# The rounds of attention written out in a new order: values' product first, q and k product in two pieces, high and low parts one round later, hT in three buffers

## The reference

```python
h = layernorm(x); h = h * (scale + 1) + shift          # scale, shift, gate from the condition
q, k, v = split_heads(h @ w_qkv)                       # 16 heads of 16
q = rope(layernorm(q, q_norm_w)); k = rope(layernorm(k, k_norm_w))
attn = softmax(q @ k.T / 4)                            # per batch and head, 256 x 256
x = x + (attn @ v) @ w_out * gate
```

## Time and profile before

| | before |
|---|---|
| median of 3 runs | 1654.78 us (1653.81 to 1656.48) |
| profiled execution | 1659.2 us, span 1657.6 us |
| TensorE busy, share of the span | 1313.8 us, 79% |
| VectorE busy | 855.8 us, 52% |
| ScalarE busy | 645.3 us, 39% |
| GpSimd busy | 324.6 us, 20% |
| mean granted clock of TensorE | 0.890 |

### The profile page before, as it was taken

The page is one execution under the profiler, slowest core; times in us unless marked ns, Lnnn a source line. Parts: engine busy times, 40 slices in busy tenths (PEclk is TensorE's granted clock), DMA queues, the critical chain, the costliest instruction groups (busy, mean ns, idle before and its releaser), DMA issues. The chain is left out here.

```text
span 1657.6 us, 37130 instructions
## 1 busy us (share of the span) xinstructions
PE 1313.8 (79%) x15240; PEld 1035.8 (62%) x15240; DVE 855.8 (52%) x1946; ACT 645.3 (39%) x1205; POOL 324.6 (20%) x311
## 2 busy tenths in 40 slices
PE   2378887887888755445149999999998999999997
PEld 2245655655656422112049999999998888888885
DVE  3656556556555245555565565655654334433432
ACT  1155565565554445544413233323322233223332
POOL 2252342442433134444300000000000000000000
PEclk8589898898897887777559999999999999999998
DMA  8112112112112300000047888888883000000000
GB/s 320 53 39 78 39 38 77 38 39 77 39 39 77 102 0 0 0 0 0 0 203 305 340 347 334 340 353 326 345 335 125 9 16 15 16 10 16 16 15 16
DMA packets 37880, 188.06 MB, mean 113 GB/s; under 512 B 3056, under 2 KB 13424, under 8 KB 29040
## 3 DMA queue, kind: packets, MB, share of 16 engines
q1 hardware_dynamic: 37744, 186.10, 29.4%
HBM read 160.66 MB, written 25.17 MB: 112 GB/s over the span
## 5 line engine op out<-in xcount | busy, mean ns | idle before, releaser
L1023 ACT ACTIVATE g<-ph,b 128x256 f32<-128x256 f32 x256 | 121.5, 475 | 276.5 <-PE ph L1186 276.4
L813 PE MATMUL pg<-XT,wfih_sb 128*128 x192 | 117.6, 777 | 102.8 <-DVE logs L898 101.0
L546 DVE TENSOR_REDUCE mx<-pR 128x4 f32<-128x1024 f32 x128 | 155.6, 1222 | 70.9 <-PE pR L673 69.6
L1376 DVE STREAM_TRANSPOSE preT<-pr 128x64 f32<-128x64 f32 x256 | 64.1, 250 | 223.8 <-PE pr L1274 223.8
L1200 PE MATMUL py<-ghi,w 128*128 128x256 f32 x512 | 147.5, 288 | 20.5 <-issue 16.2
L437 ACT ACTIVATE probs<-pR 128x1024 f32<-128x1024 f32 x128 | 131.7, 1030 | 77.0 <-PE pR L682 76.8
L1184 PE MATMUL ph<-xhi,w 128*128 128x256 f32 x512 | 146.5, 286 | 17.9 <-DMA w<-weight_halves 17.9
L1131 DVE CAST ghi<-g 128x256 fp32r<-128x256 f32 x256 | 74.8, 292 | 156.8 <-ACT g L1023 156.6
L813 PEld LDWEIGHTS pg<-XT,wfih_sb 128*128 128x128 f32 x192 | 47.4, 257 | 172.8 <-issue 172.8
L1350 ACT ACTIVATE hs<-preT 128x32 f32<-128x32 f32 x256 | 58.8, 230 | 228.6 <-DVE preT L1376 228.6
L1185 PE MATMUL ph<-xlo,w 128*128 128x256 f32 x512 | 146.0, 285 | 0.0
(11 more groups left out here) (189 smaller groups left out, 3006.5 us busy)
## 6 DMA issues: line engine op xcount, KB each, us to landing
w<-weight_halves SPq DMA_DIRECT2D x66, 2048.0 KB, 12.0
weight_halves<-wparts SPq DMA_DIRECT2D x40, 512.0 KB, 4.0
modw<-in_ew SPq DMA_DIRECT2D x32, 256.0 KB, 4.3
xn<-in_x_tok SPq DMA_DIRECT2D x4, 1024.0 KB, 12.0
XT<-in_x_dm SPq DMA_DIRECT2D x2, 2048.0 KB, 14.0
out_dm<-staged SPq DMA_DIRECT2D x16, 256.0 KB, 2.1
modw<-in_sw SPq DMA_DIRECT2D x8, 256.0 KB, 4.2
modw<-in_mod_w SPq DMA_DIRECT2D x1, 768.0 KB, 7.4
```

The source lines that it names most:

```text
L546: nc.vector.reduce_max(mx[:, :, 2 * j:2 * j + 2].rearrange("p t s -> p s t"), pR[k][:].rearrange("p s (t k) -> p s t k", t=TC), AX.X).then ...
L813: i = nc.tensor.matmul(pg[u][:, g], wfih[:, c, g * D + u * P:g * D + (u + 1) * P], XT[:, c, bass.ds(2 * p, 2)], start=(c == 0), stop=(c == ...
L1023: nc.scalar.activation(g[:, t % RING], ph[t % RING][:, 0:T], ACT.Gelu_apprx_tanh, bias=b1[:, n, f:f + 1]).then_inc(gelu_done, 1)
```

## The change

The list of fills gets a new order, all 20 rounds are written out for every engine, and each engine gets an order of its own in place of following the list:

```diff
-FILLS = [("scores_max", 0, 1), ("scores_max", 1, 1), ("scores", 0, 0), ("scores_max", 2, 1), ("scores", 1, 0),
-         ("norm_rows", 0, -1), ("scores_max", 3, 1), ("scores", 2, 0), ("out_rows", 0, -1), ("scores_max", 4, 1), ("scores", 3, 0),
-         ("project", 0, -1), ("scores_max", 5, 1), ("scores", 4, 0), ("scores_max", 6, 1), ("scores", 5, 0), ("qk_raw", 0, 3),
+FILLS = [("scores_max", 0, 1), ("scores_max", 1, 1), ("scores", 0, 0), ("norm_rows", 0, -1), ("scores_max", 2, 1), ("scores", 1, 0),
+         ("scores_max", 3, 1), ("scores", 2, 0), ("out_rows", 0, -1), ("scores_max", 4, 1), ("scores", 3, 0), ("qk_raw", 0, 3),
+         ("scores_max", 5, 1), ("scores", 4, 0), ("scores_max", 6, 1), ("scores", 5, 0), ("project", 0, -1),
          ("scores_max", 7, 1), ("scores", 6, 0), ("scores", 7, 0)] + [("qk_rows", i, 2) for i in range(4)]
-        hT = sb(st, "hT", [P, 2, DC, T])
+        hT = sb(st, "hT", [P, 3, DC, T])
```

TensorE (the waits inside are as before):

```diff
+                if has(r, 1):
+                    values_of(r + 1)
+                maxima(0)
+                maxima(1)
+                weights(0)
+                if has(r, -1):
+                    rows_of_o()
+                maxima(2)
+                weights(1)
+                if has(r, 3):
+                    rows_of_x(r + 3)
+                maxima(3)
+                weights(2)
+                if has(r, -1):
+                    out_rows()
+                maxima(4)
+                weights(3)
+                if has(r, 3):
+                    qk_raw(r, 0)
+                maxima(5)
+                if has(r, 3):
+                    qk_raw(r, 1)
+                weights(4)
+                maxima(6)
+                weights(5)
+                if has(r, -1):
+                    project()
+                maxima(7)
+                weights(6)
+                weights(7)
+                if has(r, 1):
+                    rows_of_max()
...
+                    rows_of_qk(r, 0)
+                    rows_of_qk(r, 1)
+                if has(r, 0):
+                    values(QUADS - 1)
+                if has(r, 2):
+                    rows_of_qk(r, 2)
+                    rows_of_qk(r, 3)
```

ScalarE (each line stands under its `has`):

```diff
+                    copy_v(r + 1, 1 - par)
+                    exponential(r, 0)
+                    high_parts(r)
+                    exponential(r, 1)
+                    modulate(r + 3)
+                    exponential(r, 2)
+                    save(r, 0)
+                    more_high_parts()
...
+                    nc.scalar.copy(oT[:].rearrange("p c t -> p (c t)"), pR[k][:, 0]).then_inc(free[k], 1)
...
+                    exponential(r, 3)
+                    save_raw(r)
+                    exponential(r, 4)
+                    save(r, 1)
+                    squares(r)
+                    exponential(r, 5)
+                    exponential(r, 6)
+                    save(r, 2)
+                    root(r + 3)
+                    exponential(r, 7)
+                    max_row(r)
+                    evacuate_qk(act, nc.scalar.copy, r, par, 1)
+                    evacuate_qk(act, nc.scalar.copy, r, par, 3)
...
                     save(r, QUADS - 1)
```

VectorE (the same; `scale_qk` now waits for `ya_ready` of the batch before in place of its `slots_pool`):

```diff
+                    normalise(r + 3)
+                    maxima(r, 0)
+                    maxima(r, 1)
+                    divide(r)
+                    for j in range(2, 7):
+                        maxima(r, j)
...
                     sums_of_squares(r + 3)
...
+                    add_projection(r)
+                    maxima(r, 7)
+                    negated_maxima(r)
+                    evacuate_qk(dve, nc.vector.tensor_copy, r, par, 0)
+                    scale_qk(r + 3)
+                    evacuate_qk(dve, nc.vector.tensor_copy, r, par, 2)
+                if r == -3:
                     for q in range(1, 4):
                         dve.wait_ge(x_in[q], 16)
                         token_norms(4 * q, 4 * q + 4)
```

GpSimd: the rotation of batch r+3 is at the end of round r, and the low parts of batch r+2 at its start:

```diff
                 if has(r, 2):
-                    rotate(r + 2)
+                    low_parts(r + 2)
                 for n in range(2 * (r + 3), 2 * (r + 4)):
                     split_piece(pool, n)
+                if has(r, 3):
+                    rotate(r + 3)
...
             def rotate(b):
...
                 pool.wait_ge(y_ready, b + 1)
-                if later(b):
+                if b > 0:
                     pool.wait_ge(slots_act, 3 * b)
+                    pool.wait_ge(slots_pool, b)
```

More of the change, by code:

```diff
@@ L243, in attention @@
         qk_groups = qkraw[:].rearrange("p t (g e) -> p (t g) e", e=HD)
[L244 to L258, removed]
+        ROUNDS = range(-3, B + 1)
         def has(r, ahead):
-            return not isinstance(r, int) or 0 <= r + ahead < B
+            return 0 <= r + ahead < B
         def await_full(eng, r, kind, j=0):
@@ L310, in _ @@
                 load_piece(sp, n)
-            rounds(None, one)
+            for r in ROUNDS:
+                one(r, r % 2)
             sp.wait_ge(max_moved, 32 * B)
@@ L350, in rotate, with low_parts @@
                 nc.gpsimd.tensor_tensor(yav, yav, yb[:].rearrange("p t q h j -> p (t q) h j"), ALU.add).then_inc(ya_ready, 1)
+                assert s.n == 3, s.n
+            def low_parts(b):
                 pool.wait_ge(hi_ready, b + 1)
[L353 to L357, removed]
+                nc.gpsimd.tensor_tensor(slots[:, :, 0, :, HD:2 * HD], ya[:, :, 0], slots32[:, :, 0, :, 0:HD], ALU.subtract).then_inc(half_low, 1)
+                nc.gpsimd.tensor_tensor(slots[:, :, 1, :, 2 * HD:3 * HD], ya[:, :, 1], slots32[:, :, 1, :, 0:HD], ALU.subtract)\
+                    .then_inc(slots_pool, 1)
+            for r in ROUNDS:
+                one(r, r % 2)
         @block.scalar
@@ L463, in one @@
+                if has(r, 0):
+                    exponential(r, 7)
+                if has(r, 1):
+                    max_row(r)
+                if has(r, 2):
+                    evacuate_qk(act, nc.scalar.copy, r, par, 1)
+                    evacuate_qk(act, nc.scalar.copy, r, par, 3)
                 if has(r, 0):
                     save(r, QUADS - 1)
-            rounds(act, one)
+            for r in ROUNDS:
+                one(r, r % 2)
         @block.vector
@@ new lines, in add_projection @@
+            def add_projection(r):
+                await_full(dve, r, "project")
+                dve.wait_ge(xT_in, 48)
+                k = bank_of("project")
+                for c in range(DC):
+                    xv = XT[:, c, r - 1]
+                    i = nc.vector.scalar_tensor_tensor(out=xv, in0=pR[k][:, 0, c * T:(c + 1) * T],
+                                                       scalar=modT[:, 2 * DC + c, r - 1:r], in1=xv, op0=ALU.mult, op1=ALU.add)
+                    i.then_inc(half_projected if c == 0 else free[k], 1)
@@ L599, in scale_qk @@
                 assert s.n == ROOT - 1, s.n
-                if later(b):
-                    dve.wait_ge(slots_pool, b)
+                if b > 0:
+                    dve.wait_ge(ya_ready, b)
                 nc.vector.tensor_tensor(y[:].rearrange("p t q h e -> p (t q h) e"), qk_groups,
                                         rs[:].unsqueeze(2).broadcast_to([P, TC * 2 * HEADS, HD]), ALU.mult).then_inc(y_ready, 1)
-            rounds(dve, one)
+            for r in ROUNDS:
+                one(r, r % 2)
         @block.tensor
@@ L633, in rows_of_x, with values_of @@
                 i.then_inc(x_rows, 1)
-            def values_of(b, par, last):
-                pe.wait_ge(hT_ready, b + 1 if last else b + 2)
-                if later(b):
+            def values_of(b):
+                pe.wait_ge(hT_ready, min(b + 2, B))
+                if b > 0:
                     pe.wait_ge(v_ready, b)
@@ L641, in values_of, with qk_raw @@
                     for c in range(DC):
-                        i = nc.tensor.matmul(pA[:, t * D:(t + 1) * D], hT[:, par, c, t * P:(t + 1) * P], wqkv[:, c, 2 * D:3 * D],
+                        i = nc.tensor.matmul(pA[:, t * D:(t + 1) * D], hT[:, b % 3, c, t * P:(t + 1) * P], wqkv[:, c, 2 * D:3 * D],
                                              start=(c == 0), stop=(c == DC - 1))
                 i.then_inc(v_done, 1)
-            def qk_raw(r, par):
-                bank, done = filling(r, "qk_raw")
-                pe.wait_ge(hT_ready, r + 4)
-                if not later(r + 3):
-                    pe.wait_ge(dve_ready, 2)
-                for t in range(TC):
-                    for c in range(DC):
-                        i = nc.tensor.matmul(bank[:, t], hT[:, par, c, t * P:(t + 1) * P], wqkv[:, c, 0:2 * D],
-                                             start=(c == 0), stop=(c == DC - 1))
-                i.then_inc(done, 1)
+            def qk_raw(r, t):
+                if t == 0:
+                    filling(r, "qk_raw")
+                    pe.wait_ge(hT_ready, r + 4)
+                    if r + 3 == 0:
+                        pe.wait_ge(dve_ready, 2)
+                k = bank_of("qk_raw")
+                for c in range(DC):
```

(42 more changed lines are left out.)

186 lines of the change are left out of this document (76 added, 110 removed).

## The result

The changed kernel takes 1636.0 us (median of 4, 1635.0 to 1637.7) against 1654.3: a ratio of 0.9888, 95% interval 0.9871 to 0.9905. It is faster, but by 18 us and not by the 66 forecast, and it lies outside the range. The profiled execution took 1636.7, its span is 1635.1 us, 22.5 less than before. The spans differ by more than the medians, because the profiled execution of the kernel before was 4.4 us above its median.

The account below looks back on a forecast made before the run. A round was taken as bound by the TensorE-VectorE handshake, not by an engine. Savings of 44.4 + 3.5 + 4.5 + 3 + 11 = 66.4 us gave 1588.4 us by the median; range 1573 to 1604, to 1626 with rival A.

Parts of the forecast that it names:

- normalising 0.64: VectorE at the head of a new round: normalising takes 0.64 us, read from the old trace.
- the layout of the new round: Times of one full round on all engines: 26.7 us with 2.8 of waiting, taken as 27.1 with small gaps.
- TensorE waits 0.55: Head of the new round: TensorE waits 0.55 us for reduction 0, ending at 3.55, before transposing oraw.
- rival C: Slower: rotation beside VectorE's normalising and reductions takes twice its 5.3 us, round 34.6, total 1690 us; chance 0.04.
- Full rounds: Rounds 1 to 12: each falls from 30.8 to 27.1 us, 44.4 us saved in all.
- rival A: The clock goes on falling once a round: rounds of 27.1 + 2.7, less 0.3 to 0.8, total 1624 us; chance 0.20.
- The ramp: Before round 0: token norms move behind scale_qk(0), so round 0 starts near 89.1 for 100.9; 11 us taken.
- They then run 33 to 51, beside GpSimd: In the ramp: the moved token norms, 18.1 us, run from 33 to 51 us while GpSimd splits and rotates.
- Round 0: First round of attention, without oraw transposes, output rows or projection: 27.5 to 23.7 us, 3.5 taken.
- Round 13: Round without qk product or rows of x: from 28.9 to between 23 and 25 us, 4.5 taken.
- At no cost: Moves of wx and wh loads, row of maxima and low parts cost nothing; nothing taken for leaving out the loops.
- Rivals B and C: B: only the ramp gains; rotation 2.5 us longer, high_parts late, round stays 30.8, total 1643 us; chance 0.06.

Follow-up runs that it names:

- e1: Changed kernel with VectorE normalising batch r+4 behind the negated maxima, not r+3 at the round's head: 1592.1 us, ratio 0.9605 to the kernel before.
- e5: As e1, with the token norms of batches 4 to 15 in one call instead of three: 1582.9 us, ratio 0.9565 to the kernel before.
- e9: Changed kernel with normalising as scalar_tensor_tensor instead of tensor_scalar at the same place: 1645.7 us, ratio 0.9939 to the kernel before.

## Why the prediction was wrong

**The step that failed** is the term "normalising 0.64" in the layout of the new round. By it VectorE was free at about 1.1, before the first maxima were ready, so that normalising lay under the values' product at no cost and "TensorE waits 0.55". Normalising takes 3.2 us there, because the same layout had put GpSimd's rotation at -0.7 to 4.6, over it, and TensorE waits 2.2. The duration was read from the earlier trace rows, where GpSimd stood still. A row gives a duration in its surroundings, and the surroundings were part of the edit.

The prediction came near it in rival C. It asked whether rotation would grow beside normalising, cited the Trainium skill ("GPSIMD Engine Reference", "1. Specifications") that GpSimd shares its SBUF interfaces with VectorE, noted that no row showed the two together, and then priced the wrong side. The runs show VectorE to wait and GpSimd to be delayed by 0.05. What this section of the Trainium skill names is VectorE instructions with two SBUF inputs or in a two-port mode. In these runs `tensor_tensor` and `scalar_tensor_tensor` with two SBUF inputs waited, which agrees; `tensor_scalar` with two scalar columns waited too, and no row tells whether it ran in a two-port mode. C's own sum is also off: 27.1 and 5.2 are 32.3 a round, not 34.6, unless the clock falls as well, which it doesn't say.

**Full rounds**: 44.4 forecast, 17.9 in the span. Of the 26.5 missing, by rounds without a fall of the clock, 12 x (28.2 - 26.9) = 15.6 are the wait itself, and 12 x (29.3 - 28.2) = 13.2 the clock, which falls in seven of twelve rounds behind the longer wait; 2.4 come back, as the layout was slower by 0.2 a round than e1 (26.4 in all). So rival A happened as a consequence and in part, not in its own right: at e1's waits the clock holds, with the same three banks in turn. That A's round (27.1 + 2.7, less 0.3 to 0.8) comes near the 29.3 measured is luck, as its sum leaves the long wait out. Without the contention the layout was right to 1% (27.1 and 26.9), each wait at its place.

**The ramp**: 11 forecast, 3.6 lost. "They then run 33 to 51, beside GpSimd" is the same error: they run from 33.3 to 58.7. The hT of batch 1, the q and k rows and round -1, which has normalising of 3.17 us and a clock fall of its own, all follow; e1 brings back 12.4 of the 15.4 missing and e5 8.4 more, so that round 0 begins at 83.7, before the 89.1 laid out.

**Round 0**: 3.5 forecast, 0.2 measured, and not the contention alone: in e1 it still takes 26.7 at a clock of 0.87. Taking the missing products (3.4) off a full round left out that the clock was not yet steady. **Round 13** 2.8 for 4.5 (clock 0.80), **the rest of attention** 2.5 for 3.

**At no cost**: right for wx and wh (first split at 34.3, before 35.07; nothing in the last stage), for the row of maxima and the low parts. The written-out rounds were taken as nothing. In the full rounds they are (369.2 us for 369.5); the kernel before gains 7 us with them elsewhere, from a cause that stays open.

**Rivals B and C**: ScalarE's `high_parts` waits 1.1 us for `ya` in e1, where 0.5 was laid out, and rotation takes 5.3; neither decides.

## What to carry to other kernels

When a step is moved, list what runs beside it at the new place on the other engines, for VectorE above all on GpSimd, and take its duration from a row with the same neighbour; if there is none, bound it by the neighbour's own duration: a 0.17 us instruction lasted 2.3 us. Put VectorE's SBUF work where GpSimd is idle, or where its delay has cover, and merge small instructions that must run beside it. When a kernel is bound by handshakes, a wait at one place can cost twice, once by itself and once by the clock behind it: here 1.3 and 1.1 us a round.

## What the runs showed of the hardware

Normalising and the small instructions of the token norms, started while a GpSimd `tensor_tensor` ran, ended just behind it, within 0.2 us: normalising of 256 columns took 0.41 us alone and up to 2.46 beside, 8-column instructions 0.17 and up to 2.26. This held for three forms (`tensor_scalar`, `tensor_tensor`, `scalar_tensor_tensor`). Statistics instructions, though they read SBUF, and reductions from PSUM were not touched. GpSimd's long product took 2.40 us for 2.35, and 2.54 in e9. In every such case GpSimd's instruction had begun first. The one instruction in the rows that began ahead of GpSimd's, by 0.02 us (42.10), took its usual 0.17. No row here has a long VectorE instruction begin first.

The granted clock held at 1.00 through twelve rounds with four waits of 0.5 to 0.9 us in 26.9 (e1). It fell in seven of twelve rounds that had one wait of 2.2 us among them (the changed kernel), and in ten of twelve with one of 2.5 (e9).
